# Eight opening steps of an attention half moved among the last heads and the closing steps of the one before

## What is computed

```python
x = x + jnp.tanh(g_xattn[0]) * _L0_xattn_ref(_layernorm(x, axis=-1), ctx_1024, ctx_1024, ..., mask_SxS2_bk0)
x = x + jnp.tanh(g_ffn[0]) * _L0_ffn_ref(_layernorm(x, axis=-1), ...)
x = x + jnp.tanh(g_xattn[1]) * _L1_xattn_ref(...)   # 16 heads of 8, softmax temperature from a small network
x = x + jnp.tanh(g_ffn[1]) * _L1_ffn_ref(...)       # 4 gated experts, 512 wide, 2 chosen
x = x + jnp.tanh(g_xattn[2]) * _L2_xattn_ref(...)   # 16 heads of 8, key padding mask
x = x + jnp.tanh(g_ffn[2]) * _L2_ffn_ref(...)       # 8 gated experts, 352 wide, 2 chosen
x = x + jnp.tanh(g_xattn[3]) * _L3_xattn_ref(...)   # one head
x = x + jnp.tanh(g_ffn[3]) * _L3_ffn_ref(...)       # 8 linear experts, 2 chosen
```

## Time and profile before

| what | us |
|---|---|
| median of 3 runs (lowest, highest) | 1136.41 (1135.51, 1141.63) |
| the profiled execution | 1137.24 |
| its span, first to last instruction | 1135.5 |
| PE busy, DVE busy, ACT busy, POOL busy | 944.7, 711.9, 459.6, 105.9 |

### The profile page before, as it was taken

How to read it: one execution, slowest core, us unless ns; L and a number is a source line. 1 busy time by engine, 2 the same in 40 slices (tenths; PEclk the granted TensorE clock), 3 DMA queues, 4 the chain that set the end, 5 groups by cost and what they waited for, 6 DMA issues and landing times.

```text
span 1135.5 us, 14471 instructions
## 1 busy us (share of the span) xinstructions
PE 944.7 (83%) x4795; PEld 624.7 (55%) x4795; DVE 711.9 (63%) x2190; ACT 459.6 (40%) x1101; POOL 105.9 (9%) x175
## 2 busy tenths in 40 slices
PE   2468899887777886987899899999999888979967
PEld 1434444433333355656567667666767666657744
DVE  0871433517538369579585665776776578887845
ACT  1515345455647645645635316335325222212110
POOL 3100000002103013012000100100100100000000
PEclk8669789999678898998999989999999899999987
DMA  9300000000000000000000000000000000000000
GB/s 262 118 1 1 1 1 1 1 1 1 0 1 1 1 1 1 1 1 1 1 1 2 1 1 1 1 1 1 1 1 1 1 1 10 1 10 1 1 10 9
DMA packets 12065, 12.72 MB, mean 11 GB/s; under 512 B 3758, under 2 KB 7896, under 8 KB 11992
## 3 DMA queue, kind: packets, MB, share of 16 engines
q10 hardware_dynamic: 5536, 8.04, 2.4%
q1 hardware_dynamic: 6072, 3.24, 1.1%
q0 software_dynamic: 384, 0.53, 0.3%
HBM read 10.75 MB, written 1.05 MB: 10 GB/s over the span
## 4 chain that ended last, share of the span: by engine, by line
PE 53%; DVE 28%; ACT 6%; issue 5%; POOL 2%; POOLq 0%; ACTq 0%; DVEq 0%
PE bank L1597 9%; PE bank L1585 5%; PE bank L1507 5%; PE bank L1587 4%; PE bank L1586 4%; PE bank L1392 4%; PE bank L1522 4%; DVE x L1302 3%; DVE hb L1286 3%; DVE nm L1142 3%; DVE hb L1277 3%; DVE x L1266 2%; PE bank L1562 2%; ACT PTs L946 2%; PE bank L1568 2%
## 5 line engine op out<-in xcount | busy, mean ns | idle before, releaser
L983 ACT ACTIVATE hb<-bank 96x512 f32<-96x512 f32 (+1 forms) x160 | 95.5, 597 | 262.6 <-PE bank L1587 261.7
L1585 PE MATMUL bank<-parts,m_w_lo 128*96 128x512 f32 (+1 forms) x320 | 151.0, 472 | 37.0 <-DVE hb L1277 30.0
L1597 PEld LDWEIGHTS bank<-m_w,hb 128*128 128x128 f32 (+1 forms) x1280 | 166.2, 197 | 26.8 <-issue 11.9
L1597 PE MATMUL bank<-m_w,hb 128*128 128x128 f32 (+1 forms) x1280 | 178.8, 284 | 0.5
L1286 DVE SCALAR_TENSOR_TENSOR hb<-hb,bank 96x512 f32<-96x512 f32 (+1 forms) x160 | 108.9, 680 | 87.8 <-ACT hb L983 87.4
L1587 PE MATMUL bank<-parts,m_w_hi 128*96 128x512 f32 (+1 forms) x320 | 128.9, 403 | 0.0
L1586 PE MATMUL bank<-parts,m_w_hi 128*96 128x512 f32 (+1 forms) x320 | 128.7, 402 | 0.0
L1277 DVE TENSOR_TENSOR hb<-hb,bank 96x512 f32<-96x512 f32 (+1 forms) x160 | 109.8, 686 | 11.5 <-PE bank L1587 6.4
L1585 PEld LDWEIGHTS bank<-parts,m_w_lo 128*96 128x96 f32 (+1 forms) x320 | 60.3, 189 | 82.6 <-DVE hb L1277 47.2
L1522 PE MATMUL bank<-Qs,KT 112*77 112x512 f32 x192 | 96.6, 520 | 6.8 <-ACT PTs L946 5.6
L1018 DVE RECIPROCAL rden<-bank 128x16 f32<-128x16 f32 x48 | 12.2, 255 | 130.8 <-PE bank L1345 130.8
(11 more groups left out here) (272 smaller groups left out, 1544.0 us busy)
## 6 DMA issues: line engine op xcount, KB each, us to landing
m_w<-in_L_ffn_w_dram ACTq DMA_DIRECT2D x2, 1024.0 KB, 11.4
nat_m<-in_L_ffn_W_dram ACTq DMA_DIRECT2D x1, 1408.0 KB, 16.7
x<-in_x_dram SPq DMA_DIRECT2D x4, 256.0 KB, 8.1
out_dram<-x SPq DMA_DIRECT2D x4, 256.0 KB, 2.0
f_out<-in_L_ffn_Wout_dram POOLq DMA_DIRECT2D x8, 64.0 KB, 7.9
m_w<-in_L_ffn_W_experts_dram ACTq DMA_DIRECT2D x1, 512.0 KB, 17.1
ctxn<-in_ctx_dram SPq DMA_DIRECT2D x4, 38.5 KB
Wq<-in_L_xattn_Wq_dram SPq DMA_DIRECT2D x2, 64.0 KB
```

The source lines that it names most:

```text
L983: act.activation(hb[n % 3][0:m, :], bank[UP[u, n]][0:m, :], ACT.Tanh, scale=0.5).then_inc(*chunk_act.up(u, n))
L1585: pe.matmul(dst, w_lo, x_hi, start=True, stop=False)
L1597: op = pe.matmul(bank[7][:, t * P:(t + 1) * P], hb[n % 3][0:m, t * P:(t + 1) * P], wd, start=i == 0 and t == 0, stop=ends_expert(k, n) and ...
```

## The change

Steps p0, p1 and p2 of A(i+1) are drawn after b13, b14 and b15 of A(i), and p3 to p7 after t0 to t4, for i = 0 to 10; p8 follows t6 as before. The order at a junction without feed-forward steps is then b13 p0 b14 p1 b15 p2 b16 t0 p3 t1 p4 t2 p5 t3 p6 t4 p7 t5 t6 p8 p9. The step weights follow, and the 8 steps leave the list of the unit that they belong to (that of A0 stays whole). x is transposed into bank 1 in place of bank 2 for layers 0 to 2 (`XA`), the values' product goes to free columns of bank 0, ahead of the keys' product, and its copy on ACT stands ahead of the keys' copies. The query product that goes to bank 0 waits for that copy. No arithmetic is added or removed.

```diff
--- before.py
+++ after.py
@@ -675,6 +675,9 @@
     S1 = S0 + NS
     RING = (1, 0, 2, 3)
     TURN = (4, 5)
+    BESIDE_HEADS, BESIDE_TAIL = 3, 5
+    EARLY = BESIDE_HEADS + BESIDE_TAIL
+    XA = {"A3": 2, "F3": 2}
     LATE = 2
 
     def ends_expert(k, n):
@@ -710,7 +713,13 @@
         k = kind(u)
         if k in MHA:
             block, after = (1.8, 0.8) if k == "A1" else (0.5, 0.6)
-            return [1.0] * S0 + [block] * NS + [after] * (steps_pre(k) - S1) + [0.75] * steps_body(k) + [0.6] * steps_tail(k)
+            pre = [1.0] * S0 + [block] * NS + [after] * (steps_pre(k) - S1)
+            if u[1] + 1 == ATTENTIONS:
+                heads, tail = [0.75] * steps_body(k), [0.6] * steps_tail(k)
+            else:
+                heads = [0.75] * (steps_body(k) - BESIDE_HEADS - 1) + [0.5] * 2 * BESIDE_HEADS + [0.75]
+                tail = [0.5] * (steps_tail(k) + BESIDE_TAIL)
+            return pre[EARLY if u[1] else 0:] + heads + tail
         return [1.0] * (steps_pre(k) + steps_body(k))
 
     def steps_f(u):
@@ -761,10 +770,18 @@
 
     def run(pre, body, tail):
 
+
         def attention():
+            ahead = pre(("A", 0))
             for i in range(ATTENTIONS + 2 * STREAMS):
-                u = ("A", i)
-                yield from chain(pre(u), body(u), tail(u))
+                yield from ahead
+                ahead, left = pre(("A", i + 1)), steps_body(kind(("A", i))) + steps_tail(kind(("A", i))) - 1
+                for _ in chain(body(("A", i)), tail(("A", i))):
+                    yield
+                    left -= 1
+                    if i + 1 < ATTENTIONS and 0 < left <= EARLY + 1 and left != BESIDE_TAIL + 1:
+                        next(ahead)
+                        yield
 
         def feed_forward():
             yield from pre(("F", 0))
@@ -851,7 +868,7 @@
 
                 def normalized():
                     act.wait_ge(*x_turned.at(u, T - 1))
-                    act.activation((xfa if half == "A" else xff[s])[:], bank[2 if half == "A" else UP[u, "x"]][:], ACT.Copy, scale=m2_rms[:, 0:1] if k == "F2" else 1.0) \
+                    act.activation((xfa if half == "A" else xff[s])[:], bank[XA.get(k, 1) if half == "A" else UP[u, "x"]][:], ACT.Copy, scale=m2_rms[:, 0:1] if k == "F2" else 1.0) \
                         .then_inc(*xf_ready.up(u))
 
                 for i in range(steps_pre(k)):
@@ -864,14 +881,14 @@
                             if u[1]:
                                 act.wait_ge(*keys_ready.at(("A", u[1] - 1), J - 1))
                             act.wait_ge(*k_psum.at(u))
+                            act.wait_ge(*v_psum.at(u))
+                            act.activation(VP[:, :, 0:HD],
+                                           bank[0][0:S2, G * S2:G * S2 + P].rearrange("p (h d) -> p h d", d=HD), ACT.Copy,
+                                           scale=mk[b][:, 1:2] if l == 2 else 1.0).then_inc(*values_ready.up(u))
                             for g in range(G):
                                 act.activation(Ksp[:, g, :].bitcast(F32R), bank[0][0:QK, g * S2:(g + 1) * S2], ACT.Identity,
                                                bias=bcol[0:QK, l, 1, g:g + 1],
                                                accum_out=ksum[0:QK, g:g + 1] if l == 1 else None).then_inc(*k_high.up(u, g))
-                            act.wait_ge(*v_psum.at(u))
-                            act.activation(VP[:, :, 0:HD],
-                                           bank[1][0:S2, 0:P].rearrange("p (h d) -> p h d", d=HD), ACT.Copy,
-                                           scale=mk[b][:, 1:2] if l == 2 else 1.0).then_inc(*values_ready.up(u))
                         if i == 4:
                             normalized()
                         if Q0 < i <= Q0 + G:
@@ -1350,7 +1367,7 @@
                 half, s, k, y = u[0], side(u), kind(u), stream(u)
                 l = int(k[1])
 
-                c, xn, xf = (2, xna, xfa) if half == "A" else (UP[u, "x"], xnf, xff[s])
+                c, xn, xf = (XA.get(k, 1), xna, xfa) if half == "A" else (UP[u, "x"], xnf, xff[s])
 
                 def transpose_x():
                     free(c)
@@ -1374,14 +1391,12 @@
                         if i == 2:
                             free(0)
                             pe.wait_ge(*ctx_ready.at(y))
+                            pe.matmul(bank[0][0:S2, G * S2:G * S2 + P], ctxT[y][:], Wv[l][:], start=True, stop=True) \
+                                .then_inc(*v_psum.up(u))
                             for g in range(G):
                                 op = pe.matmul(bank[0][0:QK, g * S2:(g + 1) * S2], WkR[l][:, g, :], ctxT[y][:], start=True, stop=True)
                             op.then_inc(*k_psum.up(u))
                             reader[0] = (k_low, u, G - 1)
-
-                            free(1)
-                            pe.matmul(bank[1][0:S2, 0:P], ctxT[y][:], Wv[l][:], start=True, stop=True).then_inc(*v_psum.up(u))
-                            reader[1] = (values_ready, u)
                         if i == 3:
                             transpose_x()
                         if Q0 <= i < S0:
@@ -1389,6 +1404,8 @@
                             b = RING[g % 4]
                             pe.wait_ge(*xf_ready.at(u))
                             free(b)
+                            if b == 0:
+                                pe.wait_ge(*values_ready.at(u))
                             pe.matmul(bank[b][0:QK, :], WqR[l][:, g, :], xf[:], start=True, stop=True).then_inc(*q_psum.up(u, g))
                             reader[b] = (q_low, u, g)
                         if S0 <= i < S1:
```

## The result

The changed kernel takes 1076.72 us, median of 4 runs (1072.05 to 1081.66), against 1136.32 us for the kernel before: a ratio of 0.9466, 95% interval 0.9417 to 0.9515. The profiled execution took 1072.05 us (span 1070.3), against 1137.2 (1135.5), a gain of 65; it is the fastest of its four, so some 5 us of the 65 are scatter.

A forecast was written before the change was run, and what follows sets the result against it. PE was busy 944.7 of 1135.5 us, with two chains one behind the other at early junctions. Junction gains 5.2 + 3.2 + 8.9 + 4.8 + 1, less 2 for clock, gave 21.1 us: 1116.1, or 1115.3 as median; range 1099 to 1130.

The forecast's parts named there:

- The costs where the steps now stand: At each junction, the moved steps cost 0.8 + 1.5 + 0.86 + 0.86 = 4.0 us, 4.5 at the first three.
- queries 2: In the closing part, this query product (step p7) stands ahead of the output product on PE and costs 0.86 us.
- displaced feed-forward work: Feed-forward products leaving the openings of junctions 1 to 6 must stand elsewhere at full cost, 20.4 us in all.
- PE's idle time in the openings: At junctions 7 to 10 PE is nearly full, so the gain is at most its idle time, 9.4 us.
- a new wait of 7.2: At junctions 7 to 10 PE stands at p8 until DVE updates x: 2.1 us at three, 0.9 at 7.
- the bound of 1085: Whole kernel, most gain: displaced work and the delay at seven junctions vanish in PE's idle time, a gain of 52.
- The slow clock: In closing parts the clock is 0.88 and 0.74; queries may still run at half rate, so 2 us taken off.
- a rival with 0.13: At junctions 0, 1, 3 and 4 queries run at half rate, taking 14 us off: 1129; chance 0.13.
- Displaced work hides: Feed-forward work leaving the openings fills waits of blocks and heads: 1102 us; chance 0.17.
- Only the bare junctions gain: Junctions 0, 3 and 4 gain, nothing is won beside experts but new waits stay: gain 4, 1133; chance 0.14.
- Slower: PE stands at p8 behind DVE's late x update, at 3.4 us more per junction 1146 us; chance 0.07.

The follow-up runs named there:

- the old weights: All 8 steps moved as in the change, but every step keeps its weight from the kernel before: 1103.17 us, ratio 0.9677 to the kernel before.
- fillers: Kernel before with nothing moved, plus idle 128x308 bf16 products on PE in the waits of each junction: 1142.57 us, ratio 1.0046.
- the one with the beat turned back: Changed kernel with a block step of A6 and A7 weighing 1.6 in place of 1.8: 1102.58 us, ratio 0.9675 to the kernel before.

## Why the prediction was wrong

**The direction and the mechanism at a junction were right.** Emptying the opening gains, and PE's waits in the closing part take the steps that were forecast for each. Junction 0 was to go from 17.4 to about 12 us and went to 9.9. The costs where the steps now stand were put at 4.0 us, with the attention's chain delayed by 1.5 and queries 2 on the path at 0.86 among them. In the kernel before the last weighing starts at 104.21, and the transpose of `att` 3.54 us later; in the changed kernel it starts 4.44 us later, so the delay is 0.9. From there to the output product it was 1.40 us and is now 2.41, so queries 2 cost 1.0, about as forecast. The forecast of 42.5 us less over junctions 0 to 6 (the gains of the sum, with the 20.4 us of displaced work put back into them) met 49.8; single junctions are off by up to 3.4 us either way.

**First failed step: the displaced feed-forward work was counted as costing its whole time elsewhere.** That was 20.4 us at junctions 1 to 6. Up to A7 the stages gain 54.1 us (38.9 and 15.2), and the junctions there 49.8, so what lies between became 4.3 us shorter, with all the displaced work in it (and with the closing part of A7, which belongs to junction 7 and grew by 3.6). Against the forecast that is 24.7 us, the largest part of the error. At the old weights, where the openings are emptied as well, the same sum is 23.0 us for the stages less 45.3 for the junctions: what lies between grew by 22.3, about the 20.4 that were counted. The sum treated two parts as independent that are one: what the work costs in its new place depends on which steps it lands between, and the weights decide that.

**Second: the deal itself, which the prediction did not cost at all.** It went through the steps that move and left out what the weights that "follow" do to blocks and heads. With the steps moved, the new deal makes the difference between 170.4 and 150.2 us in A6 and A7, and taking back one weight of the blocks loses 17.8 us there. Set beside the 22.3 us longer and the 4.3 shorter above, this is what turned the first step from a cost into a gain. The waits of 0.75 us on DVE explain under half of what the beat is worth in A6 and A7; for the rest the cause is open.

**Third: junctions 7 to 10 were capped by PE's idle time in the openings**, 9.4 us, less a new wait of 7.2. Their closings and openings shrank by 32.5 us and the rest of A8 to A11 grew by 22.4 (26.0 if the closing part of A7 is counted to the stage ahead). The net 10.1 of the two profiles may be a low reading: the profiles of the four kernels with nothing moved (one of them with fillers) have 321.1 to 337.7 us there, those of the nine with three steps or more moved 306.6 to 314.0. PE at 0.88 busy was no proof of a full PE: the work that stood there could move into waits of heads and blocks, as it could earlier. The mistake is the same as the first, in the form of a bound, and the bound of 1085 shared it; so the truth lay outside the bounds as well.

**The new wait was forecast to size, and mattered less.** At junction 8 PE waits 1.97 us for the x update, forecast 2.1; at 0 it is 0.94, and 13.4 in all. That its removal gains nothing shows that what is queued behind it was not on the path that sets the end, or found its next wait.

**The slow clock was off in sign.** Two us were taken off, and a rival with 0.13 had 14 lost. The merged parts run at 1.00, with 1.8 us of half clock in the junctions where there were 34.1. By the run with fillers, that alone is worth some 2 us, net of what the fillers cost.

**The rivals.** "Displaced work hides" at 1102 was the nearest, and even it gave the hiding half its size. "Only the bare junctions gain" fell: each of the 11 junctions became shorter, by 4.4 us at least. "Slower" fell, since the wait for DVE was nowhere above 1.97 us, and 1.2 us in the mean over all 11.

**What stays open.** How much of the 60 us comes by way of the clock outside the junctions: there the time at half clock fell from 165 to 109 us. Fillers tested the clock inside the junctions alone. And the parts cannot be added up: at the old deal the move gains 3.3%, at the new one 5.0%.

## What to carry to other kernels

When two streams of work are interleaved by hand on in-order engines, look for the first step of the next chain that is listed behind the last step of the one before without needing it: here the first two steps (statistics and context) drawn some microseconds earlier brought 4.0%, the third (normalizing, keys and values) 1.2% more, and the five after them nothing. Work that an emptied stretch sends elsewhere should be priced by the waits that it meets there, not by its own time. Where a planner's weights change along with a move, compare the two orders step by step first: one weight of one stretch was worth 18 us in that stretch and some 25 over the kernel, of a gain of 60.

## What was not expected of the hardware

- The scatter of one kernel goes with its clock. The changed kernel ran at 1072.05, 1072.88, 1080.56 and 1081.66 us with mean granted clocks of 0.948, 0.944, 0.936 and 0.936. Over 74 runs of 13 kernels, each against its own mean, 0.01 of clock goes with 6.4 us (correlation -0.88). If that held between kernels too, the 0.029 between the profile of before (0.912) and the mean of the changed kernel's runs (0.941) would answer to some 19 of the 60 us; it does not hold for all of them: the kernel with fillers has a mean clock of 0.927 and takes 1143 us, and the one with the beat turned back has 0.924 and takes 1103. No run separates whether the clock leads here or follows from fewer waits.
- Half clock is not bound to sparse stretches. In the blocks and heads beside experts, PE is mostly busy and yet the clock falls at places that differ from profile to profile: 0.76 from 452.7 to 464.5 us in the kernel before, with PE busy 11.0 of 11.8 us, and 1.00 behind the same block in the changed kernel (401.90 to 411.90, above). The row of the kernel before:

```profile
452.70:464.50 11.80, 11.04 (x58) 8.67 (x58) 9.19 (x39) 7.38 (x13) 0.70 (x1) 0.76 0.00 1
```

- Removing four fifths of the half-clock time of the junctions by filler made the kernel no faster: 1.0046, for 348 more products.
